# Joined parts, half blocks for the experts' remainders, another order in the relational part, and ScalarE in the first norm

## The reference

```
x = x + gated_graph(norm(x), adj)           # 3 rounds of message passing with a GRU cell
x = x + experts_relu(norm(x))               # 8 experts 128->512->128, each token in its best 2
x = x + relational(norm(x), nodemask, adj)  # one product, a sigmoid gate, a sum over neighbours, relu
x = x + experts_gelu(norm(x))               # as before with gelu, and norm inside the experts too
```

## Time and profile before

| | us |
|---|---|
| median of 3 runs (1390.91 to 1391.9) | 1390.92 |
| the profiled execution | 1389.81 |
| its span, first to last instruction | 1387.9 |
| busy PE / DVE / ACT / POOL in it | 901.5 / 928.7 / 792.0 / 768.3 |
| mean granted TensorE clock, share of full speed | 0.782 |

### The profile page before, as it was taken

How to read it: one execution, slowest core, us unless ns; L and a number is a source line. 1 busy time by engine, 2 the same in 40 slices (tenths; PEclk the granted TensorE clock), 3 DMA queues, 4 the chain that set the end, 5 groups by cost and what they waited for, 6 DMA issues and landing times. The chain is left out here.

```text
span 1387.9 us, 22286 instructions
## 1 busy us (share of the span) xinstructions
PE 901.5 (65%) x5441; PEld 474.4 (34%) x5442; DVE 928.7 (67%) x2432; ACT 792.0 (57%) x1337; POOL 768.3 (55%) x735
## 2 busy tenths in 40 slices
PE   2138788878885159999990355555550689999900
PEld 1125444434442124445540122222230235555400
DVE  4987799999998337777771345666654457777715
ACT  0366677767674147888880244544451568888800
POOL 3321133576875677777774011366665777777740
PEclk9558999999997569999996555555555799999955
DMA  9313301021110165543332311122111465443319
GB/s 227 121 61 108 106 32 32 15 51 36 42 47 26 38 146 115 136 93 84 82 78 84 117 32 32 45 65 70 41 33 40 88 137 118 92 88 87 73 49 314
DMA packets 218104, 113.84 MB, mean 82 GB/s; under 512 B 150236, under 2 KB 203630, under 8 KB 217232
## 3 DMA queue, kind: packets, MB, share of 16 engines
q1 hardware_dynamic: 189312, 72.20, 22.3%
q0 software_dynamic: 18176, 34.14, 7.2%
q10 hardware_dynamic: 10512, 6.29, 1.7%
HBM read 43.85 MB, written 53.18 MB: 70 GB/s over the span
## 5 line engine op out<-in xcount | busy, mean ns | idle before, releaser
L621 POOL DMA_INDIRECT slots<-ROWS,pos x256 | 268.0, 1047 | 91.4 <-issue 71.9
L1398 POOL DMA_INDIRECT results<-e1ys,e1home x156 | 168.7, 1082 | 47.6 <-issue 43.9
L1398 POOL DMA_INDIRECT results<-e2ys,e2home x156 | 168.2, 1079 | 47.5 <-issue 43.3
L1282 POOL TENSOR_TENSOR a_Z<-a_Z,a_H 128x512 f32<-128x512 f32 x48 | 72.8, 1516 | 150.8 <-ACT a_Z L1013 150.5
L1463 ACT ACTIVATE e1hf<-psum,VT 128x512 f32<-128x512 f32 x156 | 107.2, 687 | 74.1 <-PE psum L352 60.9
L1481 DVE SCALAR_TENSOR_TENSOR e1hs<-e1hf,e1hs 128x512 f16<-128x512 f32 x156 | 104.1, 689 | 61.8 <-ACT e1hs L1468 60.6
L1481 DVE SCALAR_TENSOR_TENSOR e2hs<-e2hf,e2hs 128x512 f16<-128x512 f32 x156 | 106.1, 703 | 54.1 <-ACT e2hs L1468 52.6
L1463 ACT ACTIVATE e2hf<-psum,VT 128x512 f32<-128x512 f32 x156 | 107.2, 689 | 38.0 <-PE psum L352 24.2
L1666 POOL TENSOR_TENSOR c_rs<-c_var,mhalf 128x12 f32<-128x12 f32 (+2 forms) x19 | 37.8, 1990 | 151.9 <-DVE c_var L1923 119.5
L350 PE MATMUL psum<-a_hT,WHH 128*128 128x512 f16 x144 | 59.0, 410 | 52.2 <-ACT a_Z L1013 41.6
L1468 ACT ACTIVATE e2hs<-e2hf 128x512 f16<-128x512 f32 x156 | 92.8, 621 | 0.0
(11 more groups left out here) (350 smaller groups left out, 2652.0 us busy)
## 6 DMA issues: line engine op xcount, KB each, us to landing
c_G<-results SPq DMA_DIRECT2D x32, 256.0 KB, 3.2
d_G<-results SPq DMA_DIRECT2D x32, 256.0 KB, 6.1
slots<-slots SPq DMA_DIRECT2D x16, 264.0 KB
W<-in_L_ffn_W_dram SPq DMA_DIRECT2D x16, 256.0 KB, 3.4
kept<-a_cut SPq DMA_DIRECT2D x16, 256.0 KB, 2.6
slots<-ROWS,pos POOLq DMA_INDIRECT x256, 2.3
W<-kept SPq DMA_DIRECT2D x2, 2048.0 KB, 10.1
out_dram<-X ACTq DMA_DIRECT2D x16, 256.0 KB, 5.9
```

The lines of the kernel that those rows point to most:

```text
L621: pool.indirect_dma_start(out=slots, out_offset=bass.IndirectOffsetOnAxis(ap=k["pos"][:, c, t:t + 1], axis=0), in_=k["ROWS32"][:, t, :], i ...
L1282: pool.tensor_tensor(Z[p % 2][:, :], Z[p % 2][:, :], H[p][:, :], ALU.mult).then_inc(zh_sb, 1)
L1398: pool.indirect_dma_start(out=k["results"][m], out_offset=bass.IndirectOffsetOnAxis(ap=home[:, GT * b + q:GT * b + q + 1], axis=0), in_=ys ...
```

## The change

Five edits:

- **Joined parts.** gated_graph and experts 1 become one Block, and relational and experts 2 another. Between the two, PE, ACT, DVE and SP drain and meet at a semaphore `over`; POOL does not take part, and only waits for it ahead of the carried sends. All Blocks are made without the drain of POOL at their end.
- **Half blocks.** 24 blocks of 512 rows (FULL) are taken for whole blocks only. What remains goes into 24 half blocks of 256 rows (HALVES), which may belong to different experts. Two of them make one pass of the loop, so there are 24 + 12 = 36 passes (NBLK) in place of 39. In the last 12 each product, each function and each bias is done in two pieces of 256 columns, and each load and tag read in two DMAs. `late_table` makes two tables.
- **Order in relational.** DVE does `mixture`(s) first. ACT does `sig` after `norms_c` and `weigh`. Both choices are made in the same step, and ranked in it; the batch is placed one step later. There are 22 steps, and sends begin in step 7, so relational sends 96 and passes on 32.
- **First norm.** In every second group DVE only computes a shift and ACT normalises in 4 activations. The moments of the next odd group wait for it (`act_norm`).
- Semaphores live as long as their Block, and those of the stored results are the program's.

```diff
+    FULL = (2 * TOK - E * (BLK - 1)) // BLK // RING * RING
+    HALVES = (2 * TOK - FULL * BLK + E * (HALF - 1)) // HALF
+    HALVES += -HALVES % (2 * RING)
+    NBLK = FULL + HALVES // 2
...
+        phase(nc, (setup, ins, k))
+        phase(nc, (first_norm, ins, k))
+        phase(nc, (gated_graph, ins, k, sent[0][0]),
+              (experts, k, "1", ACT.Relu, C_B1A, C_B2, 0, sent[0], CARRIED_1))
+        phase(nc, (relational, ins, k, sent[1][0]),
+              (experts, k, "2", ACT.Gelu, C_B1B, C_B2 + E, 1, sent[1], CARRIED_2))
+        combine(nc, k)
...
+        block = keep.enter_context(nc.Block(no_gpsimd_drain=True))
+        for n, (run, *args) in enumerate(parts):
+            if n:
+                hand_over(block, over)
+            run(nc, block, keep, over, *args)
...
+def hand_over(block, over):
+    @block.tensor
+    def _(pe):
+        pe.drain().then_inc(over, 1)
+        pe.wait_ge(over, 4)
...
             def stats(g, p):
+                if p:
+                    wait_from(dve, act_norm, g // 2)
...
             def norms(g, p):
+                if p:
+                    dve.wait_ge(lns[3], g + 1)
+                    dve.scalar_tensor_tensor(out=shift[p][:, :], in0=mv[p][:, :, 0], scalar=-1.0, in1=rstd[p][:, :],
+                                             op0=ALU.mult, op1=ALU.mult).then_inc(shifted, 1)
+                    return
...
             def his(g, p):
+                if p:
+                    act.wait_ge(shifted, g // 2 + 1)
+                    wait_from(act, lo, g - 1)
+                    for q in range(GT):
+                        i = act.activation(norm[p][:, q, :], tile_of(X, GT * g + q), ACT.Identity,
+                                           bias=shift[p][:, q:q + 1], scale=rstd[p][:, q:q + 1])
```

In experts, the loop, the pieces of a pass, POOL's wait, and as examples the up product and the function:

```diff
+        LOOPS = (FULL // RING - 2) // 2
...
+        def parts(b):
+            if isinstance(b, int) and b >= FULL:
+                return [(2 * b - FULL + h, slice(h * HALF, (h + 1) * HALF)) for h in range(2)]
+            return [(b, slice(0, BLK))]
...
+            pool.wait_ge(over, 4)
             for n in range(first, N_ALL):
                 pass_on(n)
...
+                for h, (e, (at, cols)) in enumerate(zip(es, parts(b))):
+                    t = passes(pe, HB[c][:, cols], lambda s: W1[:, s, bass.ds(e * HID + c * P, P)],
+                               lambda s: turned_rows(b, j, h)[:, s, :], h == 0, True)
...
+                    for e, cols in pieces:
+                        t = act.activation(hf[c][:, cols], HB[c][:, cols], func,
+                                           bias=VT[:, bass.ds(e * CH + b1_col + c, 1)], scale=1 / PS)
```

In relational, ACT's step and then DVE's. Beside this PE's `rank` and ACT's `weigh` go from `batch_at(s, 1)` to `batch_at(s, 0)`, DVE's `place` from 2 to 1 and its `second_choice` from 1 to 0:

```diff
-                if 0 <= s - 1 < NG:
-                    sig(s - 1, (s - 1) % 2)
                 if 0 <= s - 2 < NG:
                     v_his(s - 2, s % 2)
...
+                if 0 <= s - 1 < NG:
+                    sig(s - 1, (s - 1) % 2)
                 if 0 <= s - 2 < NG:
                     general(s - 2, s % 2)
                     relu(s - 2, s % 2)
```

```diff
+                if s < NG:
+                    mixture(s, s % 2)
                 if 0 <= s - 1 < NG:
                     los_a(s - 1, (s - 1) % 2)
                 if 0 <= s - 4 < NG:
                     los_c(s - 4)
-                if s < NG:
-                    mixture(s, s % 2)
```

More of the change, by code:

```diff
@@ L134, in program, with phase @@
         sent = [[ctx.enter_context(nc.semaphore(f"sent{m}_{part}")) for part in ("early", "late")] for m in range(2)]
[L136 to L145, removed]
-    had = list(nc.free_semaphores)
-    run(nc, *args)
+        stored = [[ctx.enter_context(nc.semaphore(f"stored{m}_{j}")) for j in range(RING)] for m in range(2)]
+        k = locals()
+        phase(nc, (setup, ins, k))
[5 more added lines that the diff above has]
+        combine(nc, k)
+def phase(nc, *parts):
+    had = list(nc.free_semaphores)
+    with ExitStack() as keep:
+        over = keep.enter_context(nc.semaphore("over"))
+        block = keep.enter_context(nc.Block(no_gpsimd_drain=True))
[3 more added lines that the diff above has]
+            run(nc, block, keep, over, *args)
     used = sorted(had[:had.index(nc.free_semaphores[0])])
-    if not used:
-        return
-    with nc.Block() as block:
+    with nc.Block(no_gpsimd_drain=True) as block:
         @block.gpsimd
@@ L159, in _, with setup @@
                     first = b
-def setup(nc, ins, k):
+def hand_over(block, over):
[3 more added lines that the diff above has]
+        pe.wait_ge(over, 4)
+    @block.scalar
+    def _(act):
+        act.drain().then_inc(over, 1)
+        act.wait_ge(over, 4)
+    @block.vector
+    def _(dve):
+        dve.drain().then_inc(over, 1)
+        dve.wait_ge(over, 4)
+    @block.sync
+    def _(sp):
+        sp.drain().then_inc(over, 1)
+        sp.wait_ge(over, 4)
+def setup(nc, block, keep, over, ins, k):
     X, ADJ, MASK = k["X"], k["ADJ"], k["MASK"]
@@ L171, in sem @@
         def sem(name):
-            return ctx.enter_context(nc.semaphore(name))
+            return keep.enter_context(nc.semaphore(name))
         V = sb("V", [P, P], F32)
@@ L405, in staggered, with first_norm @@
         step(s, s % ring)
-def first_norm(nc, ins, k):
+def first_norm(nc, block, keep, over, ins, k):
     X, ROWS, NG, ident, banks = k["X"], k["ROWS"], k["NG"], k["ident"], k["banks"]
@@ L505, with __init__ @@
 class Route:
-    def __init__(self, nc, ctx, k, tag, T, room=None):
+    def __init__(self, nc, ctx, keep, k, tag, T, room=None):
         def sb(name, shape, dt=F32):
@@ L1311, in sem @@
         def sem(name):
[L1312 removed]
+            return keep.enter_context(nc.semaphore("e" + tag + name))
         ring = range(RING)
         label = sb("label", [P, NBLK * GT, 4], I32)
[L1316 removed]
+        chosen, part = (sb(n, [P, 2 * RING, GT // 2], F32) for n in ("chosen", "part"))
         share = sb("share", [P, NBLK * GT], F32)
@@ L1456, in step @@
             def step(b, j, i, v):
-                e = act.value_load(owner[0:1, bass.ds(b, 1)], min_val=0, max_val=E - 1)
+                pieces = [(owner_of(act, at), cols) for at, cols in parts(b)]
                 wait_from(act, yT_ps, b - RING + 1)
@@ L1586, in sem @@
         def sem(name):
-            return ctx.enter_context(nc.semaphore("c_" + name))
+            return keep.enter_context(nc.semaphore("c_" + name))
         two = range(2)
```

209 lines of the change are left out of this document (125 added, 84 removed).

## The result

The changed kernel takes **1290.65 us** (median of four runs, 1286.16 to 1291.26) for 1390.91: a ratio of 0.9274, 95% interval 0.9251 to 0.9297. (All ratios here compare only executions in the chip's faster state, so a ratio can differ a little from the quotient of the two medians.) The forecast was 1272 with a range of 1250 to 1302: the direction was right and the time is inside the range, but 18.7 us above the forecast. The profiled execution took 1286.16 us with a span of 1283.9.

What follows compares the result with a forecast made beforehand. No engine was full overall: PE and POOL in step bound the experts, a ring of waits relational. Terms summed to -118.5 from 1389.8, giving 1271.3; with the median 1.1 above the profiled execution, 1272 us, range 1250 to 1302.

Steps and rivals of the forecast that it cites:

- Half blocks, forecast +2.4: Expert parts: 24 half-block passes cost 0.1 us more each, as weight loads stay hidden; +2.4 us, ends 0 and +31.
- the prediction's own sign of being wrong: Expert parts: half passes above 6.5 us would show the forecast wrong; 5.6 to 5.8 us would show it right.
- rival 1: Expert parts: ACT's pieces, SP's double loads or weight loads make half passes 1.2 to 1.3 us longer; 1300 us, 12%.
- its sum: Whole kernel: total if each of 48 matmuls in a half pass carried 25 ns more, 29 us in all: 1301 us.
- Three passes fewer, -33.6: Both expert parts: three passes fewer in each, at 5.6 us a pass with PE and POOL in step; -33.6 us.
- Relational, -61.3: Relational: shorter steps from the new order, earlier start and shorter tail; -61.3 us, ends -50 and -75.
- The new rings: Relational: waits that set a step of 10.7 us, or 12.3 with a choice; POOL sets 13.4 with sends; before 16.78.
- the tail: End of relational: one step fewer, but 6 x 4 sends and the early table; -3 us, ends 0 and -10.
- Joins and drain, -18.2 and -6.6: Part borders: POOL's 9.48 and 9.27 us idle nearly vanish, -18.2; no drain ahead of relational and combine, -6.6 us.
- Rival 3: Joins: the 9 us are the scatters' landing, not the drain, and SP's wait brings them back; 1297 us, 10%.
- Four sends, -5.0: Start of experts 2: 32 carried sends in place of 36, four fewer at 0.96 + 0.30 us; -5.0 us.
- First norm, +3.8: First norm: waiting for ACT's four normalisations costs pairs of groups without a weight piece 0.95 us; +3.8, ends 0 and +6.

Runs made afterwards that it cites:

- early reads: Changed kernel with VectorE normalising every first-norm group again, and PE in half passes reading owners once, in the middle of an earlier pass: 1264.11 us.
- whole blocks only: Changed kernel with 39 whole blocks in each expert part and the late table of before, all else as changed: 1296.16 us.
- Both single undoings: Changed kernel with one old order in relational: VectorE's (los_a and los_c ahead of mixture), 1303.06 us; or ACT's (sig ahead of v_his and norms), 1324.64 us.
- that of the slow machine: Changed kernel with every owner read of PE in a half pass done twice, eight for four, run where the kernel before took 1545 us: 1520.92 us.

## Why the prediction was right, and where it failed

- **Half blocks, forecast +2.4: this step failed.** They cost 28 us by the total and 33 by the trace, and the prediction's own sign of being wrong is there: half passes above 6.5 us. It was rival 1 in size and place (1300), but not in cause. The step costed the matmuls' columns, the weight loads, ACT's pieces and SP's transfers, and was right on all four: matmuls 0.11 apart, a pair of ACT pieces 0.73 us from its start to the next instruction's (0.76 forecast), SP ahead of PE, clock 1.00. It put at nothing what stands in PE's own queue and is no matmul, the owners' reads, 0.64 us each and twice as many in a pass of half blocks, with less matmul time queued in front (the first read starts 0.9 to 1.0 us ahead of the transposes, in full passes 1.8 to 2.5). The trace of the kernel before had them already: in the window of the earlier trace rows the source line L1409 lists 50 reads of 0.30 us, two a block.
- **Weight loads** ("TensorE: Matmul & The Clock Gate", Back-to-back issue gap, in the Trainium skill): the extra 25 ns for each of 48 matmuls are not there, starts stay 0.11 apart. The page's 81 and 56 ns are for 128 columns; carrying their difference to 256 was an estimate of the prediction. That its sum would have been nearer the time (1301) is chance: the gap is in one piece at the start of the pass and goes with the reads.
- **Three passes fewer, -33.6**: 33.4 once the gap is nearly gone (early reads against whole blocks only). POOL and PE are in step as described, and when PE fell back to 7.2, POOL waited (21 of 62.7 us).
- **Relational, -61.3**: from the first to the last root -61.9. The new rings hold by their parts: 10.5 for 10.7, 12.3 for 12.3, 13.2 for 13.4, the start -8.7 for -8.6; the tail up to the last root gave only 0.8 for 3. POOL was late next, as named. Both single undoings fit the rings.
- **Joins and drain, -18.2 and -6.6**: together -24.8 for 20 to 21 us measured, but put down wrongly: all of it is the drain and none the joining. The idle of 9.48 us in the earlier trace rows was read as the border; it was the drain at the border. Rival 3, that the 9 us come back through SP's wait, is out.
- **Four sends, -5.0**: too small. Between the last root and the second part's first result call the traces have 48 sends where there were 56, so 8 x 1.26 = 10.1 us went from there, four of them carried and four from the tail. With the join this stretch is 21.0 us shorter (83.9 to 62.9), where the sum had 14.0 for it; that is most of the 7 us by which relational with its join beat the forecast.
- **First norm, +3.8**: 2.5 to 2.7 by the stretch, the mechanism as told.

The total came out inside the range partly by luck. The expert parts missed their terms by 28 us. Relational with its join was 7 us better than forecast, gated with its join 3, and the other parts and the start 3.5 together, which leaves about 15 in the profiled execution; the median stands 4.5 above it where 1.1 was taken, and that makes 18.7. Without the parts that did better, the time would have been near 1303, just outside the range.

## What to carry to other kernels

Halving a block doubles everything that is issued once for a block and not for a column, so count what each queue holds besides its busy rows (register reads above all; the view by source line lists them), and give the reads a place where matmuls are queued in front. When a step is a ring of waits, walk the ring by single durations for each order; it was right within 0.3 us here, but the first steps and the tail have to be walked too. Ask of an idle stretch at a border whether it belongs to the meeting or to the drain of the engine, since the remedy differs.

## What the runs showed of the hardware

- A register read from SBUF takes 0.64 us of PE's queue, of which the read itself is 0.30 (four reads in a pass of the changed kernel, eight in that of the slow machine). With eight, a gap of 3.3 us was followed, 0.7 us later, by some 3 us at the lower clock; after gaps of 1.2 to 1.4 us in the changed kernel the clock stayed at 1.00.
- A transposing DMA of 256 rows takes as long on SP's queue as one of 512, so half blocks double that queue's time. In the changed kernel, durations in ns (least, median, most) from 560 to 640 us, whole blocks with five half ones among the 17 (the twelve whole ones are 1.25 to 1.30 us), and from 660 to 700 us, half blocks:

```profile
L1461 SPq DMA_TRANSPOSE e1xT<-slots x17: 1187/1252/1301, 560.5 to 639.7; - x17
```

```profile
L1461 SPq DMA_TRANSPOSE e1xT<-slots x12: 1186/1214/1672, 659.7 to 693.0; - x12
```

- The kernel before took 1545 us in one set of runs and 1390 to 1391 in the others; in the slow set PE has stalls for "issue" in the middle of passes. What causes them is open, and so is whether they belong to a chip: the record gives the same chip number, 3, to the slow set and to one of the sets at 1390.
